# Attention stacks of 64 rows in the two halves of the TensorE array, row scores issued ahead of the transposed scores, constant rows written by GpSimd

## The reference, cut to what matters

```python
# layer 0: 461 columns, own keys masked, context biased by -2
w = jnp.einsum('bhtd,bhsd->bhts', qh, kh) / jnp.sqrt(jnp.float32(Dh))
w = w * b - NEG * (1.0 - b)
w = w * stm - NEG * (1.0 - stm)
w = w + CONTEXT_ATTN_BIAS * ctx_mask
probs = jax.nn.softmax(w, axis=-1)
a = jnp.einsum('bhts,bhsd->bhtd', probs, vh)
# layer 1: 361 columns, no mask, since Sq != Sk
scores = jnp.einsum('bhqd,bhkd->bhqk', query, key) / jnp.sqrt(jnp.asarray(D_K, dtype=query.dtype))
attn = jax.nn.softmax(scores, axis=-1)
x = jnp.einsum('bhqk,bhkd->bhqd', attn, value)
```

## Time and profile before

| | us |
|---|---|
| median of 3 runs | 663.76 (663.71 to 664.19) |
| span of the profiled execution | 664.1 |
| PE busy | 515.1 (78%) |
| DVE busy | 429.5 (65%) |
| ACT busy | 297.8 (45%) |
| POOL busy | 162.6 (24%) |
| layer-0 rounds | 81.8 to 271.0 |
| layer-1 rounds | 370.6 to 484.5 |

### The profile page before, as it was taken

One profiled execution on the slowest core, in us unless ns is written; L12 is line 12 of the kernel. 1 busy time (PEld: TensorE's weight loads), 2 busy tenths in 40 slices (PEclk: granted clock), 3 DMA queues, 4 the chain that ended last, 5 costly groups with the idle time before them and its releaser, 6 DMA issues. The chain is left out here.

```text
span 664.1 us, 15475 instructions
## 1 busy us (share of the span) xinstructions
PE 515.1 (78%) x5403; PEld 356.1 (54%) x5403; DVE 429.5 (65%) x921; ACT 297.8 (45%) x482; POOL 162.6 (24%) x191
## 2 busy tenths in 40 slices
PE   2477798998988898737547878998975269999994
PEld 1263365665666667523223545655654258887782
DVE  7365576667686774387754856777569875666662
ACT  6442145556556538203314546676753223333331
POOL 5500022122122211010045410122125044444432
PEclk9989588979999977668659788999976569999997
DMA  9136834444535700000073787789347111222210
GB/s 258 40 120 113 161 82 105 105 115 110 112 99 140 188 5 25 1 1 0 0 154 88 181 155 151 142 165 178 121 158 270 60 40 28 48 40 47 49 19 1
DMA packets 73247, 64.31 MB, mean 97 GB/s; under 512 B 33326, under 2 KB 65750, under 8 KB 73190
## 3 DMA queue, kind: packets, MB, share of 16 engines
q1 hardware_dynamic: 61544, 41.37, 28.3%
q0 software_dynamic: 8224, 21.06, 12.0%
q10 hardware_dynamic: 3424, 1.12, 0.8%
HBM read 48.59 MB, written 15.92 MB: 97 GB/s over the span
## 5 line engine op out<-in xcount | busy, mean ns | idle before, releaser
L467 PEld LDWEIGHTS PS<-QS,KS 112*120 112x120 f16 (+2 forms) x896 | 81.9, 144 | 29.9 <-issue 10.9
L467 PE MATMUL PS<-QS,KS 112*120 112x100 f16 (+2 forms) x896 | 92.8, 229 | 5.1 <-ACT PT L530 3.7
L578 DVE CUSTOM_DVE_ANT_0 PS<-PS,maskv 100x461 f32<-100x461 f32 x128 | 80.5, 647 | 15.2 <-PE PS L436 14.3
L581 DVE TENSOR_REDUCE mx<-PS 100x1 f32<-100x361 f32 x128 | 63.6, 529 | 35.8 <-PE PS L439 34.7
L530 ACT ACTIVATE PT<-PS 120x400 f32<-120x400 f32 (+1 forms) x128 | 63.4, 503 | 45.5 <-PE PS L467 43.1
L530 ACT ACTIVATE PT<-PS,ctxb 120x400 f32<-120x400 f32 (+1 forms) x96 | 57.0, 596 | 52.7 <-PE PS L467 51.9
L436 PE MATMUL PS<-KS,QS 65*100 65x461 f16 x128 | 52.6, 416 | 17.9 <-DVE mx L578 17.3
L795 POOL TENSOR_SCALAR_AFFINE_SELECT PT<-PT 100x400 f32<-100x400 f32 x32 | 17.7, 553 | 187.6 <-ACT PT L530 187.6
L2025 PE MATMUL PS<-aT,WE 128*128 128x128 f16 x960 | 59.4, 224 | 0.0
L2025 PEld LDWEIGHTS PS<-aT,WE 128*128 x960 | 57.0, 101 | 0.0
L2038 PE MATMUL PS<-WE,hidden_high 128*128 x160 | 53.0, 379 | 0.0
(11 more groups left out here) (307 smaller groups left out, 1069.7 us busy)
## 6 DMA issues: line engine op xcount, KB each, us to landing
share<-in_L_ffn_w_dram POOLq DMA_DIRECT2D x13, 1024.0 KB, 9.3
k_scratch<-share SPq DMA_DIRECT2D x32, 180.5 KB, 2.5
KS<-k_scratch SPq DMA_DIRECT2D x32, 180.5 KB, 3.6
KS<-k_scratch SPq DMA_DIRECT2D x64, 90.2 KB, 6.3
QS<-q_scratch SPq DMA_DIRECT2D x64, 50.0 KB, 2.7
v_scratch<-xn SPq DMA_DIRECT2D x8, 385.7 KB
values_staged<-v_scratch SPq DMA_DIRECT2D x8, 385.7 KB
WE<-in_L_ffn_w_dram POOLq DMA_DIRECT2D x2, 1024.0 KB, 8.6
```

What stands on the lines that cost most here:

```text
L467: last = nc.tensor.matmul(bank[0:kn, i * T:(i + 1) * T], KS[p][:, h, k0:k0 + kn], QS[p][:, h, :], start=True, stop=True)
L578: nc.vector.tensor_tensor_reduce(rows, rows, maskv[:, :], 1.0, -BIG, ALU.add, ALU.max, mx[p][:, h:h + 1]).then_inc(s_smf, 1)
L581: nc.vector.tensor_reduce(mx[p][:, h:h + 1], sm_bank[h % 2][0:T, 0:TC], X, ALU.max).then_inc(s_smf, 1)
```

## The change

A stack now has 64 rows: 0 to 31 hold qh twice against kh and kl, 32 to 47 the maxima against the diagonal, 48 to 63 ql against kh. The product of ql and kl is left out. Even batches lie in partitions 0 to 63, odd ones in 64 to 127, of one buffer KSa and one QSa. `pe_SM` uses all 64 rows. With 64 rows the program places these matmuls in a half of the array's rows, the lower for even and the upper for odd batches; the row scores of batch u+1 and the transposed scores of batch u are always in opposite halves.

The row scores of a step now stand right ahead of its transposed ones (in layer 1, the first of a step ahead and the second behind), and VectorE's maximum ahead of the block's work. The diagonals of both halves are written by one POOL copy, the zeros of QSa by one VectorE memset. The zero rows that the query rows 32 to 47 need at first come from there: SP writes them to DRAM in two transfers, and each stack of queries then comes in by three transfers (16, 16 and 32 rows), the keys by one of 32 rows and one of 16.

```diff
-    KROWS = 4 * DH
-    IROW = 96
-    KX = IROW + H
+    KX = 4 * DH
+    IROW = 2 * DH
...
-        KS = [KSa[0:KX, p] for p in range(2)]
-        QS = [in_all(f"QS{p}", [KX, H, T], F16) for p in range(2)]
+        QSa = in_all("QS", [P, H, T], F16)
+        KS, QS = ([a[p * KX:(p + 1) * KX] for p in range(2)] for a in (KSa, QSa))
...
-                loads = 6 * (j + o // 2 + 1) if layer == 0 else 6 * (B // 2) + 2 * (j + o // 2 + 1)
+                loads = 7 * (j + o // 2 + 1) if layer == 0 else 7 * (B // 2) + 3 * (j + o // 2 + 1)
...
-                nc.tensor.matmul(bank[0:T, 0:S0], QS[p][0:KROWS + 1, h, :], KS[p][0:KROWS + 1, h, :],
-                                 start=True, stop=True).then_inc(s_smd, 1)
...
+            n = S0 if layer == 0 else TC
+            nc.tensor.matmul(bank[0:T, 0:n], QS[p][:, h, :], KS[p][:, h, 0:n], start=True, stop=True
+                             ).then_inc(s_smd, 1)
...
             for s_ in range(2):
-                sp.dma_start(QS[o % 2][s_:KROWS:2, hs, :], src).then_inc(s_ks[o % 2][mb], 16)
+                sp.dma_start(QS[o % 2][s_:IROW:2, hs, :], q_dram[hs, 0, :, ts].rearrange("h d t -> d h t")
+                             ).then_inc(s_ks[o % 2][mb], 16)
+            sp.dma_start(QS[o % 2][IROW:KX, hs, :], q_dram[hs, 1:3, :, ts].rearrange("h a d t -> (a d) h t")
+                         ).then_inc(s_ks[o % 2][mb], 16)
...
-            for a in range(2):
-                sp.dma_start(dst[a * 2 * DH:(a + 1) * 2 * DH, hs, :], src).then_inc(done, 16)
+            sp.dma_start(dst[0:IROW, hs, :], src.rearrange("h d s t -> (d s) h t")).then_inc(done, 16)
+            sp.dma_start(dst[IROW + H:KX, hs, :], src[:, :, 0, :].rearrange("h d t -> d h t")).then_inc(done, 16)
...
                 sp_ctx(sp, 0, 1)
+                sp.wait_ge(s_kz, 1)
+                for mb in range(KC):
+                    sp.dma_start(q_dram[mb * HM:(mb + 1) * HM, 1, :, :],
+                                 QSa[:, 0:HM, :].rearrange("p h t -> p (h t)")).then_inc(s_qw, 16)
...
+                sp.wait_ge(s_kr, 1)
                 sp.wait_ge(s_kw[0][0], KW)
...
-                nc.gpsimd.memset(KS[0][KROWS:IROW, HM:H, :], 0.0)
-                nc.gpsimd.memset(KS[1][KROWS:IROW, 0:HM, :], 0.0)
-                nc.gpsimd.memset(KS[1][KROWS:IROW, HM:H, :], 0.0).then_inc(s_kz, 1)
-                pool.wait_ge(s_kz, 1)
+                nc.gpsimd.tensor_copy(KSa[:, :, :], delta[:, :].unsqueeze(2).to_broadcast([P, H, S0])).then_inc(s_kr, 1)
...
-                act.wait_ge(s_dl, 1)
-                for p in range(2):
-                    nc.scalar.activation(KS[p][IROW:KX, :, :], delta[:, :].unsqueeze(2).to_broadcast([H, H, S0]), ACT.Copy
-                                         ).then_inc(s_kr, 1)
...
                     for t in range(16):
                         if t == 4:
                             pe.wait_ge(s_vsb[u], j + 1)
+                        if nxt:
+                            pe_SM(pe, j, u + 1, t, 0, 0)
                         pe_ST(pe, j, u, t, 0, 0, 0)
...
-                        if nxt:
-                            pe_SM(pe, j, u + 1, t, 0, 0)
                         if t in PVT0:
...
-                for p in range(2):
-                    nc.vector.memset(QS[p][KROWS:IROW, :, :], 0.0)
-                nc.vector.memset(KS[0][KROWS:IROW, 0:HM, :], 0.0)
+                nc.vector.memset(QSa[:, :, :], 0.0).then_inc(s_kz, 1)
...
                     for t in range(16):
+                        if nxt:
+                            dve_max(dve, j, u + 1, t, 0, 0)
...
-                        if nxt:
-                            dve_max(dve, j, u + 1, t, 0, 0)
...
                     for t in range(NST1):
+                        sms = SMH1[t] if nxt else 0
+                        if sms > 0:
+                            pe_SM(pe, j, o + 1, h, 1, SMN)
+                            h += 1
                         pe_ST(pe, j, o, t, 1, STN, 2 * B)
+                        if sms > 1:
+                            pe_SM(pe, j, o + 1, h, 1, SMN)
+                            h += 1
                         unread()
...
-                            for _ in range(SMH1[t]):
-                                pe_SM(pe, j, o + 1, h, 1, SMN)
-                                h += 1
```

More of the change, by code:

```diff
@@ L75, in flamingo @@
     of = out.rearrange("b t d -> (b t) d")
[L79 removed]
+    q_dram = nc.dram_tensor("q_scratch", (H, 3, DH, NT), F16, kind="Internal").ap()
     sk_dram = nc.dram_tensor("own_key_scratch", (H, DH, 2, NT), F16, kind="Internal").ap()
@@ L161, in flamingo @@
         s_pad = sem("padding_cleared")
-        s_kz = sem("key_stacks_cleared")
+        s_kz = sem("query_stacks_cleared")
         s_bias = sem("biases_loaded")
@@ L434, in pe_SM @@
             bank = sm_bank[h % 2]
-            if layer == 0:
-                nc.tensor.matmul(bank[0:T, 0:S0], QS[p][0:KROWS + 1, h, :], KS[p][0:KROWS + 1, h, :],
-                                 start=True, stop=True).then_inc(s_smd, 1)
-            else:
-                nc.tensor.matmul(bank[0:T, 0:TC], QS[p][0:KROWS + 1, h, :], KS[p][0:KROWS + 1, h, 0:TC],
-                                 start=True, stop=True).then_inc(s_smd, 1)
+            n = S0 if layer == 0 else TC
+            nc.tensor.matmul(bank[0:T, 0:n], QS[p][:, h, :], KS[p][:, h, 0:n], start=True, stop=True
+                             ).then_inc(s_smd, 1)
         def pe_N(pe, j, o, smn, freed):
@@ L645, in sp_stack0 @@
             sp_queries_in(sp, j, o, mb)
-            sp_keys_in(sp, j, o, hs, KS[p][0:KROWS, :, 0:T], sk_dram, True, s_ks[p][mb])
+            sp_keys_in(sp, j, o, hs, KS[p][:, :, 0:T], sk_dram, True, s_ks[p][mb])
             if written is not None:
                 sp.wait_ge(written, count)
-            sp_keys_in(sp, j, o, hs, KS[p][0:KROWS, :, T:S0], k_dram[0], False, s_ks[p][mb])
+            sp_keys_in(sp, j, o, hs, KS[p][:, :, T:S0], k_dram[0], False, s_ks[p][mb])
         def sp_keys1(sp, j, o, g):
             p, hs = o % 2, slice(g * HG, (g + 1) * HG)
-            sp_keys_in(sp, j, o, hs, KS[p][0:KROWS, :, 0:TC], k_dram[1], False, s_kg[p][g])
+            sp_keys_in(sp, j, o, hs, KS[p][:, :, 0:TC], k_dram[1], False, s_kg[p][g])
         with nc.Block() as block:
@@ L681, in _ @@
                 sp_keys_out(sp, 0, 0, 0)
-                sp.wait_ge(s_qw, 16 * 8)
+                sp.wait_ge(s_qw, 16 * 10)
+                sp.wait_ge(s_kr, 1)
                 sp.wait_ge(s_kw[0][0], KW)
@@ L757, in _ @@
                                         base=0, pattern=[[-1, P]], channel_multiplier=1).then_inc(s_const, 1)
-                nc.gpsimd.affine_select(out=delta[:, :], in_=delta[:, :], compare_op=ALU.not_equal, fill=WS * WS,
-                                        base=0, pattern=[[-1, H]], channel_multiplier=1).then_inc(s_dl, 1)
+                for p in range(2):
+                    nc.gpsimd.affine_select(out=delta[:, :], in_=delta[:, :], compare_op=ALU.not_equal,
+                                            fill=WS * WS, base=-(p * KX + IROW), pattern=[[-1, H]],
+                                            channel_multiplier=1).then_inc(s_dl, 1)
+                    pool.wait_ge(s_dl, p + 1)
                 nc.gpsimd.affine_select(out=maskv[:, 0:T], in_=maskv[:, 0:T], compare_op=ALU.is_ge, fill=-BIG,
@@ L946, in _ @@
                         pe_K(pe, 0, o, k, n0 + 2 + k, n0 + 1)
-                pe.wait_ge(s_kr, 2)
-                pe.wait_ge(s_kz, 1)
+                pe.wait_ge(s_kr, 1)
                 for c in range(3):
@@ L1422, in flamingo @@
         NST1 = 12
-        QB = 16 * 8
+        QB = 16 * 10
         WEB = 4 * KC * DF * 2
@@ L1642, in _ @@
                 for a, half in enumerate((qh1, ql1)):
-                    act.dma_start(q_dram[HM:H, a, :, :], half[:, 1, :]).then_inc(s_qw1, 16)
+                    act.dma_start(q_dram[HM:H, 2 * a, :, :], half[:, 1, :]).then_inc(s_qw1, 16)
                 act.wait_ge(s_vz, 1)
```

16 lines of the change are left out of this document (7 added, 9 removed).

## The result

The changed kernel takes 687.86 us in the median of 4 runs (680.95 to 693.0), the kernel before in the same runs 663.98 (663.71 to 665.43). The ratio is 1.027 (95% interval 1.022 to 1.032): slower, where 652 was forecast.

A forecast was written before the change was run, and what follows sets the result against it. PE's stream of matmuls was taken as nearest the bound in both layers' rounds. The terms summed to -11.6 against the profiled span of 664.1, giving 652.5, less 0.3 for the median: 652.2 us, range 640 to 673.

The forecast's parts named there:

- the rival: Seven full-clock rounds of both layers: each gets one 1.2 GHz stretch, 18.9 us on top, 671.1 in all; chance 0.11.
- The argument against it: Against a lower clock in the full-clock rounds: they keep their clock now, with short waits in them.
- The constant rows: Prologue: without ACT's 12.58 us of constant diagonals, the first projection starts at 20.32 instead of 24.93; -4.6 us.
- ACT's part: Prologue: with ACT's constant rows gone, wah can run at about 9.6 and is done by 11.1.
- The copy at "0": POOL's copy of constant rows, estimated at 19.1 us, ends well before the first stack load needs it; cost 0.
- Overlap and changes of tile: Rounds: paired scores save 0.16 each, -13.1 in layer 0, -11.2 in layer 1; 239 tile changes at 0.11 cost +26.3.
- the 0.04 for a first weight load: Row and transposed scores side by side: 0.21 for the longer plus some 0.04 for its first weight load, 0.25.
- Order: Maxima and row scores ahead of the block's work: a third of layer 0's 13.6 us of waits goes, -4.5.
- The 3 us forecast for layer 1: New order in layer 1: a fifth of the 14.7 us of waits on weight loads goes, -3.
- Transfers: Layer 1: keys of 48 rows cut stack waits, -2; a third query transfer adds an issue before its first scores, +0.5.

The follow-up runs named there:

- e1: Changed kernel with both stacks at partition 0, zero-padded so score matmuls use all 128 array rows, and constant rows by ScalarE: 670.48 us, ratio 1.010.
- e5: Changed kernel, still in halves, with layer 1 back in the order of the kernel before: 713.82 us.
- e6: e1 with layer 1 back in the order of the kernel before: 670.26 us.
- e2: Changed kernel with 64-row score matmuls but both stacks in the lower half of the array, constant rows by ScalarE: 750.75 us.
- e8: Changed kernel with two unread full-width matmuls per layer-1 step instead of one: 673.53 us.
- e3: Changed kernel with GpSimd's copy of the constant rows held until VectorE has made the input's low halves: 678.46 us.
- e9: Kernel before with only layer 0's row scores and maxima moved to the new order: 657.26 us, ratio 0.988.
- e7: Kernel before with only layer 1 put in the new order: 667.77 us, ratio 1.002.
- e12: Changed kernel with three edits: late GpSimd copy, queries issued ahead of keys in layer 1, two unread matmuls per layer-1 step: 672.03 us.
- e11: e6 with one swap: in layer 1 SP issues a half's queries ahead of the group's keys: 647.85 us, ratio 0.974.
- e13: e11 with the constant rows moved: ScalarE writes one stack's, GpSimd the other's, late: 649.60 us, ratio 0.975.
- e14: Kernel before with layer 0's new order, constant rows moved, and layer 1's queries issued ahead of keys; stacks of 112 rows: 645.82 us, ratio 0.973.

## Why the prediction was wrong

**The failed step is the clock.** The forecast summed streams at full clock, and put a lower granted clock at 0.11, as one stretch in each of seven rounds, 18.9 us. It is what happened, and larger: layer 1 takes 24.3 us more at 0.69 instead of 0.94, and layer 0's last round, which the rival left out, 6.5 more at 0.54. The last round's loss goes with the halves (15.8 on full width, e1). Of layer 1's, 9.4 go with the halves in the new order (e1), and 25.6 in the order of before (153.9 in e5, 128.3 in e6); the rest stays on full width, for the late queries below. The rival's stated reason (fewer full arrays, more gaps) was half right: e2 shows the clock at 1.2 GHz with no gaps at all, and e8 shows it back with more full-height matmuls. The argument against it, that these rounds keep their clock before, spoke of a kernel whose scores had 65 and 112 rows.

**The constant rows (-4.6, measured +1.5 at the first projection).** ACT's part was right (wah done at 10.63, forecast 11.1). The copy at "0" was not: its cover was counted for those who need its result, not for VectorE beside it, which it held for 6.3 us. Its length was taken too long, 19.1 us for 6.33, which did no harm. e3 gets 6.6 back at the first projection.

**Overlap and changes of tile (-24.3 and +26.3).** Both mechanisms were right, and so was it that they nearly cancel. A pair saves 0.15 to 0.16, as was taken (the 0.04 for a first weight load stood there without a row; what the runs show is 0.42 for the four of `pe_ST` where it was 0.38, without its reason); a change of tile costs 0.10 on the way in and 0.09 on the way out, where 0.11 was taken. In a full-clock layer-0 round the changes cost 1.2 (e2 against e1) and the overlap gains 1.2 (after against e2). So the halves gave nothing there even at full clock.

**Order (-4.5 in layer 0).** Right, and under-sized: 0.9 to 1.0 in each full-clock round, and e9 shows that it is the whole of layer 0's gain (159.2 for its first seven rounds, 160.1 after the change, 167.6 before). The 3 us forecast for layer 1 are not seen (e7).

**Transfers (-2 + 0.5).** Wrong in sign. The bytes fell, but the third query transfer was counted as one issue more ahead of layer 1, not as one that is issued behind keys and expert weights in six rounds. In the changed kernel itself this hides behind the slow clock (7.2 us of waits, and the swap brings nothing in e12's layer 1, 125.1 for 124.3 in e8); on full width it costs 21.5 us of layer 1 (e6 against e11), 12.5 of them waits, the rest with a clock of 0.87 instead of 0.97.

What stays open: what exactly the chip counts when it lowers the clock. The runs show it lower with score matmuls of 64 rows, and higher again with more full-height ones between them, not where the limit lies, nor whether the number of rows or the placing in half the array decides, nor whether the added matmuls help by their height or by their 512 columns. Why the gains of late constant rows are partly lost again in e12 and e13 was not tried further.

## What to carry to other kernels

Ask of every change that shrinks matmuls what it does to the granted clock, not only to the stream: here work packed into half the array's rows ran at 1.2 GHz for much of layer 1, and filler of full height made it faster. Count for each moved operation who shares its memory interface and which queue it now stands in; two of the terms here went wrong by that, not by their length. When a change has several parts, try the plain ones alone: here the order of issue and the place of a load gave most of what was gained, with stacks as they were before (e14).

## What was not expected of the hardware

PE busy for 179.47 of 179.70 us at a granted clock of 0.50 (e2): being busy did not bring the clock back, while the same scores on full width had 0.83 in spite of longer waits (e1). A GpSimd copy of 6.33 us stopped a VectorE operation of 0.57 us on ten columns for its whole length, while another VectorE operation, with one of its inputs in PSUM, ran beside it unhindered.
